# Moving two tiles of the shared expert from the last stage into the output stage

## What is computed

```python
gate = xt @ Wr + br
_, ids = top_k(gate + gate_bias, 2)
probs = softmax(gate masked to ids)
u = einsum('nh,ehi->eni', xt, Wup) + bup
g = silu(einsum('eni,eij->enj', u, Wgate) + bgate) * u
eo = einsum('enj,ejh->enh', g, Wdown) + bdown
out = einsum('ne,enh->nh', probs, eo)
su = xt @ Wsu + bsu
sg = silu(su @ Wsg + bsg) * su
out = out + sg @ Wsd + bsd            # the shared expert
return x + out
```

## Time and profile before

| | us |
|---|---|
| median of 3 runs | 993.98 (993.63 to 997.36) |
| the profiled execution | 995.3 |
| its span, first to last instruction | 993.6 |
| PE busy | 909.5 (92%) |
| DVE busy | 636.0 (64%) |
| POOL busy | 563.9 (57%) |
| ACT busy | 459.5 (46%) |

### The profile page before, as it was taken

The page is one execution under the profiler, slowest core; times in us unless marked ns, Lnnn a source line. Parts: engine busy times, 40 slices in busy tenths (PEclk is TensorE's granted clock), DMA queues, the critical chain, the costliest instruction groups (busy, mean ns, idle before and its releaser), DMA issues. The chain is left out here.

```text
span 993.6 us, 16827 instructions
## 1 busy us (share of the span) xinstructions
PE 909.5 (92%) x5047; PEld 406.6 (41%) x5048; DVE 636.0 (64%) x1019; ACT 459.5 (46%) x846; POOL 563.9 (57%) x487
## 2 busy tenths in 40 slices
PE   3889895799999999989999689999999999999898
PEld 1345442122221222246644245555555555555443
DVE  7888777588787988467776144554554444443388
ACT  3375665678877888722353022332233233323540
POOL 5465556367777775543127499989999920000372
PEclk9798998599999999999999799999999999999999
DMA  7234635445454532133425766666566643335676
GB/s 233 77 92 122 179 105 166 139 158 169 167 177 159 177 105 70 53 107 128 153 112 218 289 191 209 217 200 220 201 215 205 201 139 106 121 109 187 232 203 221
DMA packets 106059, 162.26 MB, mean 163 GB/s; under 512 B 12536, under 2 KB 55608, under 8 KB 105616
## 3 DMA queue, kind: packets, MB, share of 16 engines
q1 hardware_dynamic: 92768, 115.86, 35.9%
q0 software_dynamic: 12896, 45.10, 13.6%
q10 hardware_dynamic: 336, 0.57, 0.2%
HBM read 107.88 MB, written 53.48 MB: 162 GB/s over the span
## 5 line engine op out<-in xcount | busy, mean ns | idle before, releaser
L1089 ACT ACTIVATE p_t<-a_psT 128x512 f32<-128x512 f32 x256 | 138.9, 595 | 47.4 <-PE a_psT L1212 46.1
L1136 DVE TENSOR_REDUCE nm<-quad 128x4 bf16<-128x1984 f32 x60 | 133.9, 2231 | 35.7 <-PE quad L1197 35.7
L1905 ACT ACTIVATE e_xT<-quad 128x512 f16<-128x512 f32 x38 | 22.7, 597 | 229.9 <-PE quad L1969 229.9
L1979 PE MATMUL quad<-w_exp,e_xT 128*128 x456 | 107.2, 386 | 4.9 <-DVE e_xT L1933 2.6
L1039 POOL TENSOR_TENSOR p_sum<-p_t,p_t 128x512 f32<-128x512 f32 x64 | 81.1, 1275 | 53.2 <-ACT p_t L1089 53.0
L1979 PE MATMUL quad<-w_exp,e_uT 128*128 x456 | 104.6, 379 | 0.0
L1979 PE MATMUL e_psY<-w_exp,e_gT 128*128 x456 | 104.6, 379 | 0.0
L1212 PE MATMUL a_psT<-q_stk,k_stk 98*128 98x512 f16 x256 | 84.6, 401 | 11.2 <-ACT p_t L1089 9.4
L215 POOL TENSOR_TENSOR w_exp<-e_raw,w_exp 128x1024 f16<-128x1024 f32 x42 | 91.7, 2184 | 3.5
L1936 DVE SCALAR_TENSOR_TENSOR e_g<-quad,bias 128x512 f32<-128x512 f32 x38 | 26.3, 691 | 85.4 <-PE e_psGT L1969 80.5
L1936 DVE SCALAR_TENSOR_TENSOR e_u<-quad,bias 128x512 f32<-128x512 f32 x38 | 26.3, 691 | 73.9 <-PE quad L1979 73.9
(11 more groups left out here) (338 smaller groups left out, 1797.0 us busy)
## 6 DMA issues: line engine op xcount, KB each, us to landing
xs_dram<-zero SPq DMA_DIRECT2D x38, 256.0 KB, 6.9
bias<-in_L_ffn_bup_dram SPq DMA_DIRECT2D x38, 256.0 KB, 3.3
bias<-in_L_ffn_bgate_dram SPq DMA_DIRECT2D x38, 256.0 KB, 3.4
ys_dram<-e_y SPq DMA_DIRECT2D x38, 256.0 KB, 2.0
e_x<-xs_dram SPq DMA_DIRECT2D x36, 256.0 KB, 2.8
q_dram<-q_st SPq DMA_DIRECT2D x24, 256.0 KB, 3.0
k_dram<-k_st SPq DMA_DIRECT2D x24, 256.0 KB, 3.6
q_stk<-q_dram SPq DMA_DIRECT2D x64, 96.0 KB
```

What stands on the lines that cost most here:

```text
L1089: act.activation(probs(w, k), psT[:, k % 2], ACT.Exp, scale=SCALE / (QS * QS)).then_inc(s["exp"], 1)
L1136: dve.tensor_reduce(nm[:, i, :, 0:1].rearrange("p h o -> p (h o)"), psS[:, :, 0:NMAIN], AX.X, ALU.max, negate=True)
L1979: ins = pe.matmul(dst[:, :], stationary, moving, start=(k == 0), stop=(k == len(terms) - 1))
```

## The change

NFIRST goes from 8 to 10. The output stage gets a third group of two tiles (256 tokens): 256-wide up and gate chunks and two down tiles. The ring goes by a list of chunks, CHUNKS, in place of ORDER. The bias product of the ten front tiles becomes the 13th and last matmul of their down group there, for which the output stage builds its own bd and pT: SP loads the biases six times (three parts), POOL clears bd and pT and makes low3, ACT and DVE make bd, PE turns pmat ahead of each group's down, and ACT copies the result to pT. DVE computes the group 2 gate after pmat. Buffers move to make room, and wait for what they now overlap.

```diff
-NFIRST = 8
+NFIRST = 10
...
+    WIDTH = (S, S, NFIRST * P - 2 * S)
+    u = [mid("f_u0", [P, KD, S], F32), again[0]("f_u1", [P, KD, S], F32), sb("f_u2", [P, KD, WIDTH[2]], F32)]
...
+    CHUNKS = [(kind, grp, c) for kind in "ugd" for grp in GROUPS for c in range(KD if kind != "d" else WIDTH[grp] // P)]
...
+
+            for part in range(3):
+                at = part * (E + 1)
+                sp.dma_start(bd_raw[at:at + E, :], t["L0_ffn_bdown"]).then_inc(s["bd_loaded"], 16)
+                sp.dma_start(bd_raw[at + E:at + E + 1, :], t["L0_ffn_bsd"].rearrange("(o n) -> o n", o=1)).then_inc(s["bd_loaded"], 16)
...
+            pool.wait_ge(s["x1_r"], NT)
+            pool.memset(bd[:, :], 0.0).then_inc(s["bd_const"], 1)
+            pool.wait_ge(s["xn_r"], NT)
+            for k in range(3):
+                pool.wait_ge(x1_st[k], 16 * ((NT - 1 - k) // 3 + 1))
+            pool.memset(pT[:, :, :], 0.0).then_inc(s["bd_const"], 1)
...
+                if grp == 2 and c == 0:
+                    act.wait_ge(xT_st[0], 16)
...
+            for grp in GROUPS:
+                for c in range(KD):
+                    up(grp, c)
+            act.wait_ge(s["bd_loaded"], 16 * 6)
+            act.activation(bd_hi[:, :], bd_raw[:, :], ACT.Copy, scale=WS).then_inc(s["bd0"], 1)
+            act.activation(bd_16[:, :], bd_raw[:, :], ACT.Copy, scale=WS).then_inc(s["bd0"], 1)
             act.wait_ge(s["exp_in"], 1)
             act.activation(ex[:, :, :], sel[:, :, :], ACT.Exp).then_inc(s["exp"], 1)
...
+            act.wait_ge(s["bd_const"], 2)
+            for q, n in enumerate((TB, TB, NFIRST - 2 * TB)):
+                act.wait_ge(s["pT_t"], q + 1)
+                act.activation(pT[0:K3, TB * q:TB * q + n, :].rearrange("p n t -> p (n t)"), (psR, psW)[q % 2][0:K3, 0:n * P], ACT.Copy).then_inc(s["pT_c"], 1)
...
+            for c in range(KD):
+                up_low(2, c)
+            dve.wait_ge(s["bd0"], 2)
+            dve.wait_ge(s["bd_const"], 4)
+            dve.scalar_tensor_tensor(bd[0:K3, :], bd_hi[:, :], low3[:, :], bd_16[:, :], ALU.mult, ALU.add).then_inc(s["bd1"], 1)
...
+            dve.tensor_tensor(pmat[:, :, 1, :], pmat[:, :, 1, :], ph16[:, :, :], ALU.subtract).then_inc(s["pmat"], 1)
+            for c in range(KD):
+                gated(2, c)
+                if c:
+                    gated_low(2, c - 1)
+            gated_low(2, KD - 1)
+            for grp in GROUPS:
+                for j in range(WIDTH[grp] // P):
+                    down(grp, j)
...
+                product(chunk_bank("u", grp, c)[:, 0:WIDTH[grp]], [(weight(0, y, q)[:, at], xT_all[:, grp, q, x, 0:WIDTH[grp]]) for q in range(KD)
...
+                dst = chunk_bank("d", grp, j)
+                terms = [(gT[grp][:, q, x, at], weight(2, y, q)) for q in range(KD) for x, y in ((0, 0), (1, 0), (0, 1))]
+                for i, (a, b) in enumerate(terms):
+                    pe.matmul(dst[:, :], a, b, start=(i == 0), stop=False)
+                pe.wait_ge(s["pT_c"], grp + 1)
+                pe.wait_ge(s["bd1"], 1)
+                pe.matmul(dst[:, :], pT[:, TB * grp + j, :], bd[:, :], start=False, stop=True).then_inc(s["d_mm"], 1)
...
+            def turn_probs(q, n):
+
+                pe.wait_ge(s["pmat"], 1)
+                if q >= 2:
+                    pe.wait_ge(s["pT_c"], q - 1)
+                for c in range(n):
+                    ins = pe.transpose((psR, psW)[q % 2][0:K3, c * P:(c + 1) * P], pmat[:, TB * q + c, :, :].rearrange("p a e -> p (a e)"), ident[:, :])
+                ins.then_inc(s["pT_t"], 1)
...
+            for grp in (1, 2):
+                for c in range(KD):
+                    up(grp, c)
+            for grp in GROUPS:
+                for c in range(KD):
+                    gate(grp, c)
+            for grp in GROUPS:
+                if grp < 2:
+                    turn_probs(grp, TB)
+                else:
+                    turn_probs(grp, NFIRST - 2 * TB)
+                for j in range(WIDTH[grp] // P):
+                    down(grp, j)
```

```diff
+    SPAN = ((1, slice(0, S), NT - TB), (0, slice(NFIRST * P - 2 * S, S), NFIRST))
+    WIDTH = [at.stop - at.start for _, at, _ in SPAN]
...
+    TILES = list(range(NFIRST)) + list(range(NT - TB, NT)) + list(range(NFIRST, NT - TB))
...
             def store(m):
                 if m < NFIRST:
-                    sp.wait_ge(s["p_r"], m + 1)
+                    sp.wait_ge(s["acc"], TOP * (TILES.index(m) + 1))
                 else:
-                    sp.wait_ge(s["d_r"], m - NFIRST + 1)
+                    sp.wait_ge(s["d_r"], TILES.index(m) - NFIRST + 1)
                 sp.dma_start(rows_of(out_rows, m), row(m)).then_inc(s["stored"], 16)
-            for m in range(TB):
+            for m in TILES:
                 store(m)
-            for j in range(TB):
...
-            for m in range(NT):
-                if m >= IN_FLIGHT // TOP:
-                    before = m - IN_FLIGHT // TOP
+            for n, m in enumerate(TILES):
+                if n >= IN_FLIGHT // TOP:
+                    before = n - IN_FLIGHT // TOP
                     pool.wait_ge(ready[before % len(ready)], 16 * TOP * (before // len(ready) + 1))
...
+            up(1, 0)
+            up(1, 1)
             turned_probs(0)
             turned_probs(1)
-            up(1, 0)
-            up(1, 1)
-            turned_probs(2)
-            turned_probs(3)
...
 
-            def first_total(m):
-                dve.wait_ge(s["p_mm"], m + 1)
-                total(m, psP[m % 2], s["p_r"])
-
             def down(grp, j):
                 dve.wait_ge(s["d_mm"], TB * grp + j + 1)
-                total(NFIRST + TB * grp + j, chunk_bank("d", grp, j), s["d_r"])
+                total(SPAN[grp][2] + j, chunk_bank("d", grp, j), s["d_r"])
...
-                first_total(c)
             gated_low(1, KD - 1)
+            gathered(2 * TB)
+            gathered(2 * TB + 1)
             for j in range(TB):
                 gathered(NFIRST + j)
-                first_total(TB + j)
                 down(0, j)
-            for j in range(TB):
+            for j in range(NT - TB - NFIRST):
                 gathered(NFIRST + TB + j)
                 down(1, j)
...
+                product(chunk_bank("u", grp, c)[:, 0:WIDTH[grp]], [(weight(0, y, q)[:, at], xT[:, SPAN[grp][0], q, x, SPAN[grp][1]]) for q in range(KD)
...
-                product(chunk_bank("d", grp, j), [(pT[:, NFIRST + TB * grp + j, :], bd[:, :])] + [
+                if (grp, j) == (0, 0):
+                    pe.wait_ge(s["pT_c"], 2)
+                    pe.wait_ge(s["bd1"], 1)
+                product(chunk_bank("d", grp, j), [(pT[:, TB * grp + j, :], bd[:, :])] + [
                     (gT[:, grp, q, x, at], weight(2, y, q)) for q in range(KD)
                     for x, y in ((0, 0), (1, 0), (0, 1))]).then_inc(s["d_mm"], 1)
...
+                for c in range(TURNED[q]):
...
-            def first_bias(m):
-                if m == 0:
-                    pe.wait_ge(s["pT_c"], NT // 4)
-                    pe.wait_ge(s["bd1"], 1)
-                at_least(pe, s["p_r"], m - 1)
-                pe.matmul(psP[m % 2][:, :], pT[:, m, :], bd[:, :], start=True, stop=True).then_inc(s["p_mm"], 1)
...
                 up(0, c)
+            up(1, 0)
+            up(1, 1)
             turn_probs(0)
             turn_probs(1)
-            up(1, 0)
-            up(1, 1)
-            turn_probs(2)
-            turn_probs(3)
             up(1, 2)
             up(1, 3)
             for c in range(KD):
                 gate(0, c)
-                if c >= 2:
-                    first_bias(c - 2)
             for c in range(KD):
                 gate(1, c)
-                if c:
-                    first_bias(c + 1)
             for j in range(TB):
                 down(0, j)
-                if j + TB + 1 < NFIRST:
-                    first_bias(j + TB + 1)
-            for j in range(TB):
+            for j in range(NT - TB - NFIRST):
                 down(1, j)
```

More of the change, by code:

```diff
@@ L1721, in free @@
                 if before >= 0:
-                    what, of = ORDER[before // KD]
-                    pe.wait_ge(s[{"u": "u_r", "g": "silu", "d": "d_r"}[what]], KD * of + before % KD + 1)
+                    what, of, n = CHUNKS[before]
+                    pe.wait_ge(s[{"u": "u_r", "g": "silu", "d": "d_r"}[what]], KD * of + n + 1)
                 elif q >= 4:
@@ L1741, in up @@
                 at = slice(c * P, (c + 1) * P)
-                product(chunk_bank("u", grp, c), [(weight(0, y, q)[:, at], xT_all[:, grp, q, x, :]) for q in range(KD)
+                product(chunk_bank("u", grp, c)[:, 0:WIDTH[grp]], [(weight(0, y, q)[:, at], xT_all[:, grp, q, x, 0:WIDTH[grp]]) for q in range(KD)
                                                   for x, y in ((0, 0), (1, 0), (0, 1))]).then_inc(s["u_mm"], 1)
@@ L1748, in gate @@
                 at = slice(c * P, (c + 1) * P)
```

(17 more changed lines are left out.)

130 lines of the change are left out of this document (59 added, 71 removed).

## The result

The changed kernel takes 1007.65 us (1005.31 to 1010.77); the kernel before, on the same chip at the same time, 996.50 (993.63 to 998.57). The ratio is 1.0123, with a 95% interval from 1.0104 to 1.0142: some 12 us slower. The forecast was 1002.7 us, within 995 to 1009, and slower at 0.70.

The account below looks back on a forecast made before the run. PE was taken to bound both touched stages, except a hole ending the output stage; gathers would set the last stage's new end. From 993.98 us, +15.5 - 0.4 - 6.4 = +8.7 gave 1002.7 us, range 995 to 1009 (forecast's own 999 to 1006).

Parts of the forecast that it names:

- Output stage, +15.5: Output stage: 18.8 us of added PE work, only 3.3 hidden, so the routed stage starts 15.5 us later (14.7 to 17).
- hand-over: End of output stage: last DVE addition, SP store and barrier put PE's routed start at 578.4, after its end at 575.6.
- The join, 0.2 of waits: Output stage, before the first down products: PE waits about 0.2 us for the turned probabilities, at most 1.5.
- The clock, -0.4: Routed stage's start: of 3.3 us lost to PE's half speed after the hole, 0.4 comes back; bounds 0 and 3.3.
- Last stage, -6.4: Last stage: gathers, one tile every 3.1 us, set the end; 6.4 us saved, ends -11.3 and -1.9.
- PE's hole, 4 to 6 us: Last stage: PE idles 4 to 6 us before its down products, as gated_low(0,3) follows gathered(7) on DVE; covered.
- Sum, +8.7: Whole kernel: +15.5 output stage, -0.4 clock and -6.4 last stage make +8.7 us.
- heavier contention: Rival: last-stage tiles every 3.45 us (-1.9) and 1.5 us of stalls before output-stage downs; about 1008.7 us; chance 0.17.
- unloaded pace: Rival: last-stage gathers keep their pace without stores, saving 11.3 us there; 997.8 us in all; chance 0.22.
- PE as the bound: Rival: PE sets the last stage's end, saving 18.8 us; 990.3 us; needs tiles every 2.1 us from the fifth; chance 0.06.

Follow-up runs that it names:

- the run with the join alone: Against the kernel before: NFIRST stays 8, the eight front tiles' bias products join their down products, last stage in the new order; ratio 1.0019.

## Where the prediction held and where it did not, step by step

- **Output stage, +15.5: measured +14.6.** The 256-wide matmul was taken at 0.108 and is 0.109. The Trainium skill, "TensorE: Matmul & The Clock Gate", section "Back-to-back issue gap", has 262 cycles for it, an estimate of 0.109 us at 2.4 GHz, and the trace agrees. PE ends 60.6 us after the up chunks, as the sum said (575.6 - 515.0). The term that was too large is the hand-over: 2.8 us taken, 581.16 - 579.29 = 1.9 measured. I carried over before's 1.7 us between an ACT issue and the end of the barrier; behind SP's last store it is 0.6.
- **The join, 0.2 of waits: held,** because the gates of the third group cover it. I had named that cover only in a number (546.1 and 549.4); the run with the join alone gave its price, 5.1 us and the lower clock behind it.
- **The clock, -0.4: the routed stage is 1.8 us shorter in the profile,** within the bounds of 0 to -3.3. The clock fell again behind the short gap (0.63 granted from 583.4 to 588, after a gap of 1.7 us, four transposes and 1.6 us more). But kernels with the same output stage have 360.9 and 362.2, and before's own stage 361.4 and 362.8, so the size of the change's share is not shown: the means (362.1 of the two profiles without the change, 361.3 of the eight with the third group) differ by 0.8.
- **Last stage, -6.4: measured -1.2.** This is the term that was mis-sized. The mechanism held (POOL's rule of two tiles, one store per tile, the last gather issued at 1000.08 and not before 990), and the fifth tile starts 16.4 us after the entry, as good as the 16.7 that was taken over from before. But the tiles follow every (998.44 - 958.55) / 11 = 3.63 us, where I took 3.1 and gave 3.45 as the end. "Two tiles then take 1.3 (second issue) + 4.8 (landing)" is where it fails: the chain has 1.34 + 0.30 from issue to issue, 5.2 to 5.6 until that second gather lands, and 0.26 until POOL goes on, some 7.3 us for two. About half of the missing 1.2 us are the two gaps, which the sum left out; the other half is the landing. I had taken the middle between 4.4 and 5.2, but the gather that POOL waits for, the second of the four issued in a row, takes longest of them: 5.2 to 5.6 us, as against 4.3 to 4.9 for the two behind it. Why it is this one that is slow is not shown. The rows of before had nearly all of it: with the median of 5.2 in the earlier trace rows and the two gaps the same sum gives 3.5 us a tile and -1.0 us for the stage. The shorter landing of the last one (4.15 for 4.8) gives a little back.
- **PE's hole, 4 to 6 us: 9.5 measured.** gathered(7) starts 35.5 us after the entry (977.65 - 942.18), where the 958 that I took from before's pace is 32.4. The hole is DVE's order, and PE's late end is covered, as predicted, but for at most 3.4 us.
- **Sum, +8.7: some 12.** The sum is nearer than its terms: the last stage was taken 5.2 us too short, the output stage and the clock together 2.3 us too long, and that these partly cancel is luck. Of the 5 us between 1002.7 and 1007.65, about half is the kernel before, which in these runs took 996.50 where the forecast started from 993.98. The measured time lies outside the forecast's own range (999 to 1006), in that of the heavier contention (1006 to 1010). That rival's -1.9 was close in the last stage, though its stalls in the output stage did not come. The unloaded pace gave -11.3 in the last stage: it takes three tiles in flight to reach that. PE as the bound fell at the point named for it.

## What to carry to other kernels

Before moving work off the engine that binds a stage, find the chain that is second there and work out its own end with the new order of events. For a loop of "issue, wait for the one k before, issue", take the landing time of the very transfer that is waited for, under the load that the change brings, add the gaps between issues, and see whether k can be raised; here that one number gave back nearly all that the change cost (1.0123 to 1.0019). And when a product is joined to another, look at what covers the wait for its operand: in this order it was free only because a third group of gates happened to stand in front of it.

## What the runs showed of the hardware that I had not expected

- With two tiles of gathers in flight beside stores the DMA engines moved some 197 to 237 GB/s, with three 254 to 316 (windows from 958 to 980 us), while each gather took about as long to land (4.8 and 5.2 us in the median).
- POOL mostly takes 0.95 to 1.4 us for one issue of such a gather and 0.30 until the next; 32 of them took 44 us without a wait for a landing, and with the last landing and addition that made a last stage of 54 us.
- The part ahead of the up chunks took 514.2 to 519.8 us in the profiles, the output stage behind it 62.4 to 62.5 in all eight kernels that have the third group. In these profiles most of what the code does not explain lies in the beginning of the kernel, 4.6 us of it before the output stage; stages are better compared from a common instant than by the span.
